# Keyed scores in front of query-major scores: one reordering on TensorE in a pipelined attention kernel

## The reference

```python
Qh, Kh, Vh = (split_heads(Q), split_heads(K), split_heads(V))
scores = jnp.einsum('bhqd,bhkd->bhqk', Qh, Kh) / jnp.sqrt(jnp.float32(D))
scores = jnp.where(mask == 0, jnp.float32(-1000000000.0), scores)
attn = jax.nn.softmax(scores, axis=-1)
Z = jnp.einsum('bhqk,bhkd->bhqd', attn, Vh)
```

## Time and profile before

| | us |
|---|---|
| median of three runs | 1529.95 (1526.15 to 1530.41) |
| the profiled execution's own time | 1529.28 |
| its span, first to last instruction | 1527.4 |
| outside the span | 1.88 |
| TensorE busy with matmuls, over the span | 1186.4 |
| VectorE busy | 977.2 |
| ScalarE busy | 639.0 |
| GpSimd busy | 596.7 |

### The profile page before, as it was taken

One profiled execution on the slowest core, in us unless ns is written; L12 is line 12 of the kernel. 1 busy time (PEld: TensorE's weight loads), 2 busy tenths in 40 slices (PEclk: granted clock), 3 DMA queues, 4 the chain that ended last, 5 costly groups with the idle time before them and its releaser, 6 DMA issues. The chain is left out here.

```text
span 1527.4 us, 30086 instructions
## 1 busy us (share of the span) xinstructions
PE 1186.4 (78%) x9187; PEld 789.3 (52%) x9187; DVE 977.2 (64%) x4100; ACT 639.0 (42%) x1541; POOL 596.7 (39%) x1132
## 2 busy tenths in 40 slices
PE   3789989998365479999996395884658865999778
PEld 2455555554365245565553294763655642454455
DVE  5777777773566567787772674365655655776445
ACT  2355645444222145666654043330235431666422
POOL 3553478987243344455420443322430112321120
PEclk9699999999578579999998597776787895999889
DMA  6344665530022344455420125001220014341000
GB/s 185 118 129 141 207 183 169 182 122 3 32 60 61 104 127 124 137 168 168 147 82 11 40 57 176 0 15 34 62 76 1 0 39 135 101 123 43 2 0 28
DMA packets 140014, 137.35 MB, mean 90 GB/s; under 512 B 12288, under 2 KB 109184, under 8 KB 139728
## 3 DMA queue, kind: packets, MB, share of 16 engines
q1 hardware_dynamic: 131248, 110.88, 23.9%
q0 software_dynamic: 8608, 24.55, 5.0%
HBM read 83.58 MB, written 49.18 MB: 87 GB/s over the span
## 5 line engine op out<-in xcount | busy, mean ns | idle before, releaser
L762 ACT ACTIVATE L0a_Pr<-PS 128x512 f32<-128x512 f32 (+1 forms) x256 | 136.8, 547 | 137.5 <-PE PS L664 88.4
L762 ACT ACTIVATE L1a_Pr<-PS 128x512 f32<-128x512 f32 (+1 forms) x256 | 136.2, 547 | 100.5 <-PE PS L664 50.5
L479 POOL TENSOR_TENSOR L0a_PG<-L0a_Pr,L0a_G 128x512 f32<-128x512 f32 x80 | 105.7, 1325 | 25.6 <-issue 11.0
L885 DVE CUSTOM_DVE_ANT_0 L1a_junk<-PS,L1a_neg 128x256 bf16<-128x256 f32 x256 | 94.8, 420 | 29.7 <-PE PS L637 29.4
L637 PE MATMUL PS<-L0a_Kst,Qm 128*128 128x256 bf16 (+1 forms) x512 | 94.9, 272 | 16.8 <-DVE L0a_mx L885 9.9
L637 PE MATMUL PS<-L1a_Kst,Qm 128*128 128x256 bf16 (+1 forms) x512 | 94.7, 272 | 16.5 <-DVE L1a_mx L885 9.1
L885 DVE CUSTOM_DVE_ANT_0 L1a_junk<-PS,causal_q 128x128 bf16<-128x128 f32 (+1 forms) x256 | 78.5, 352 | 37.0 <-PE PS L637 36.3
L885 DVE CUSTOM_DVE_ANT_0 L0a_junk<-PS,causal_q 128x128 bf16<-128x128 f32 (+1 forms) x256 | 78.5, 352 | 36.7 <-PE PS L637 36.0
L888 DVE TENSOR_REDUCE L3x_mx<-PS 128x2 f32<-128x512 f32 x128 | 83.8, 685 | 24.5 <-PE PS L637 24.2
L659 PE MATMUL PS<-Qm,L0a_Kst 128*128 128x512 bf16 (+1 forms) x256 | 91.5, 357 | 9.3 <-DMA Qm<-L0a_mT 6.6
L885 DVE CUSTOM_DVE_ANT_0 L0a_junk<-PS,L0a_neg 128x256 bf16<-128x256 f32 x192 | 72.9, 418 | 37.0 <-PE PS L637 36.5
(11 more groups left out here) (739 smaller groups left out, 3183.4 us busy)
## 6 DMA issues: line engine op xcount, KB each, us to landing
Qm<-q_image SPq DMA_DIRECT2D x160, 128.0 KB
sorted_in<-zeros POOLq DMA_DIRECT2D x16, 516.0 KB, 4.3
L0a_Kst<-k_image SPq DMA_DIRECT2D x64, 128.0 KB
ffn_w_<-L_ffn POOLq DMA_DIRECT2D x32, 256.0 KB, 3.5
L1a_Kst<-k_image SPq DMA_DIRECT2D x64, 128.0 KB
ffn_w_<-L_ffn SPq DMA_DIRECT2D x16, 256.0 KB, 6.3
L3x_Kst<-k_image SPq DMA_DIRECT2D x32, 128.0 KB
k_image<-L0a_kpart SPq DMA_DIRECT2D x16, 192.0 KB, 2.6
```

The source lines that it names most:

```text
L479: g.tensor_tensor(PG[:, V_ % GATED_RING, :].rearrange("p (h q) -> p h q", h=2), Pr[:, V_ % RING, :].rearrange("p (h q) -> p h q", h=2), G[ ...
L762: a(Pr[:, V_ % RING, 0:2 * nq], PS[:, T_BANK + v % 2, 0:2 * nq], ACT.Exp, scale=SCALE)\
L885: ins = v.tensor_tensor_reduce(junk[:, tt, par, 0:nk], scored[:, par], off, 1.0, LOWEST, ALU.add, ALU.max, mx[:, i % 2, tt, par, hp:hp + 1])
```

## The change

In each step of the loop on TensorE, the call of `keyed_scores` is put in front of that of `scores`. Nothing is added or removed, the waits inside the two functions move with them, and the programs of the other engines stay as they are.

```diff
+                    i, v = unit(n, TLAG)
+                    if i is not None:
+                        keyed_scores(i, v)
                     i, u = unit(n, 0)
                     if i is not None:
                         scores(i, u)
-                    i, v = unit(n, TLAG)
-                    if i is not None:
-                        keyed_scores(i, v)
                     i, x = unit(n, PV_LAG)
                     if i is not None and x % 4 == 0:
                         times_v(i, x // 4)
```

## The result

| | before | after |
|---|---|---|
| median of nine runs each, us | 1526.15 (1521.06 to 1530.41) | 1536.02 (1531.82 to 1540.96) |
| ratio after to before | | 1.0069, 95% interval 1.0048 to 1.0090 |
| the profiled execution's own time, us | 1529.28 | 1536.02 |
| its span, us | 1527.4 | 1534.2 |
| VectorE busy, us | 977.2 | 997.3 |

The kernel became 0.7% slower where I had put 1527.3, 0.2% faster than the median of 1529.95 that I started from. The surprise of the page is in VectorE's row: its program did not change, and it is busy for 20.1 us more. To find the place I took each item's period, from the end of its last E to the end of the next item's last E (items 0 to 7 are L0a, 8 to 15 L0x; the groups are counted from the end of their first E).

What follows compares the result with a forecast made beforehand. TensorE's own work was taken to bound the mixed stretches. Terms 2.7 + 0.6 - 1.9 + 1.7 + 0.9 - 1.3 + 0 gave 2.7 us gained: 1529.28 to 1526.6, or 1527.3 with the median 0.67 higher; range 1518 to 1537.

Steps and rivals of the forecast that it cites:

- The bound: Mixed attention stretches: TensorE's own work sets the pace, so only what alters its waits can move the end.
- the cost of the change: Mixed steps: no matmul added, S and T keep 640 each and their durations, and the switch costs nothing in itself.
- The third rival: Nothing moves: stream and waits turn as one, GpSimd holds L0x and gives back the rest; 1530 us, chance 0.05.
- The loop turns without moving: Mixed steps: waits of S and T neither removed nor doubled, only slightly changed; +2.7, +0.6 and -1.9 us.
- `pick_heads`: L602's wait for the copy `Osb`, which moves earlier with T: +1.7 us in causal blocks, +0.9 in L1x and L3x.
- `turn_attended`: L610's wait for `A`, whose chain starts at S and comes 0.22 us later in six cases of L0a and L1a: -1.3 us.
- The first T: First T of an item waits for the transfer of maxima, S now behind it: +0.9 and -0.9, together 0 us.
- 15.84 within 0.2: Sign: the 15.84 us between like steps of a late L0a item would stay within 0.2 of that.
- T's waits for `Pr` grown by 10 us or more: Sign in the trace after that was to prove the rival that S stands behind T's waits.
- the second rival: S stands behind T's waits: E's arrival doesn't move while S's place does; 1540.7 us, chance 0.15.
- S's total far below 56 us: Sign: with T's waits small, it would prove that T fills S's waits, a rival at 1519.6 us, chance 0.20.

Runs made afterwards that it cites:

- e1: The swap everywhere except in steps whose keyed scores belong to L0x, against the kernel before: 1523.08 us, ratio 1.0002.
- e3: Old order, GpSimd's gate products cut to 8 columns (part of the gating left out), against the kernel before: 1516.01 us, ratio 0.9946.
- e4: New order, GpSimd's gate products cut to 8 columns (part of the gating left out), against the kernel before: 1515.43 us, ratio 0.9955.
- e14: New order, GpSimd's gate products replaced by about equally long fills that read nothing, against the kernel before: 1523.56 us, ratio 0.9983.
- e15: Old order, GpSimd's gate products replaced by the same fills that read nothing, against the kernel before: 1522.17 us, ratio 0.9978.
- e5: New order, VectorE's gate product put ahead of the step's row maximum, against the kernel before: 1522.12 us, ratio 0.9981.
- e6: Old order, VectorE's gate product put ahead of the step's row maximum, against the kernel before: 1529.13 us, ratio 1.0034.
- e7: New order, VectorE's gate product one step later, still behind the row maximum, against the kernel before: 1527.30 us, ratio 1.0016.
- e8: Old order, VectorE's gate product one step later, still behind the row maximum, against the kernel before: 1526.41 us, ratio 1.0009.
- e12: Built on e4, one VectorE product in each of two items followed by five copies into spare tiles; against the kernel before: 1519.28 us, ratio 0.9968.
- e9: New order, GpSimd's expert weight transfers issued four steps later, against the kernel before: 1528.89 us, ratio 1.0034.
- e10: Old order, GpSimd's expert weight transfers issued four steps later, against the kernel before: 1511.99 us, ratio 0.9923.

## Why the prediction was wrong

- **The bound.** Right outside L0x. I called TensorE the pace of all mixed stretches, and noted GpSimd's 130.1 of 150 us in L0x only as a second engine. That it reads SBUF beside VectorE's product I didn't ask. The time of 1536.02 lies inside the range that I gave (1518 to 1537), on the side of slower: that is the width of the range, and no credit to the mechanism.
- **The step that failed** is the cost of the change: "S and T keep their counts (640 each) and durations", and nothing of any other engine's durations. L897 stands in no step of it: what the new order does to its length was put at nothing, without a reason. It went from 39.5 to 57.9 us, held M so that S waited up to 3.22 us, and behind that wait the clock fell. The third rival said that GpSimd "holds L0x (130.1 of 150) and gives back the rest"; the reverse happened: the two engines got in each other's way, and the cost moved to VectorE, which TensorE waits for (GpSimd's 80 products sum to 104.3 us, from 106.0).
- **The loop turns without moving** (+2.7, +0.6, -1.9). The mechanism held: e1 gives 1.0002, the items of L0a move by half a microsecond at most in both directions (item 5, where I had named 15.84 within 0.2, has 15.54), and items 33 to 35 of L3x are 0.21 us shorter each. The single terms are too small for what was measured.
- **`pick_heads`** (+2.6 in all). Right in the trace: L602's waits, 3.0, 4.7 and 1.8 us in the earlier trace rows, are no longer among the waits of these stretches. No time came of it that could be measured.
- **`turn_attended`** (-1.3). Right in sign, larger in number: L610 waits 4.1 us in 7 times and 5.8 in 13, from 2.5 in 3 each.
- **The first T** (0). In the case I worked through, the wait went from 0.82 to 0.67 us, 0.15 less, where I had 0.2. Over the groups it grew, from 8.2 to 9.1 us in the first, and in the second this term was mis-sized: the first T of item 17 waits 1.79 us, from 1.05. Of the changed kernel's TensorE and clock there:

```profile
...
575.88 0.39 PE L659 MATMUL PS<-Qm,L1a_Kst 128*128 128x512 bf16 x1 [1.79 <-DMA Qm<-L1a_mT]
...
```
```profile
576.00:580.00 4.00, 4.00 (x33) 2.45 (x32) 2.14 (x16) 1.79 (x3) 1.15 (x3) 0.61 0.64 202
580.00:590.00 10.00, 8.92 (x86) 5.93 (x87) 6.73 (x41) 4.42 (x11) 2.70 (x8) 0.99 0.19 65
```

  Behind the idle 1.79 us the granted clock is 0.61 over 4 us, near its 1.2 GHz level, and 0.99, the 2.4 GHz level, again behind them. Item 17 is 1.53 us longer by it, of the second group's +2.3. The wait belongs to the new order: it is 1.68 to 1.99 us in all eight kernels that have the swap there and the weights at their old step, and 1.05 to 1.17 in the six with the old order. The fall of the clock is in two of the eight, this one and e1, with 19.16 and 19.22 us for item 17; the other six have 17.48 to 17.80, as before (17.63). So the wait alone costs nothing that can be measured, and the fall costs 1.6 us when it comes. What decides whether it comes was not settled. In the median of e1 no loss is left of it.
- **The signs that I named.** "T's waits for `Pr` grown by 10 us or more" was to prove the second rival. They grew from 1.8, 2.6 and 3.7 us to 4.3, 5.8 and 11.2, by 13.2 in all, and most in L3x, which ended 0.2 us earlier. There S waits 7.1 us less and T 7.5 us more: the wait changed its name. The sign was badly chosen, as a wait that moves from one instruction to another in the same loop costs nothing. "S's total far below 56 us" didn't come: 33.4 + 16.1 + 6.3 = 55.8.
- **The second rival** had a time nearest to the result (1540.7 against 1536.0), for a reason that e3, e4, e14 and e15 exclude. That is luck.
- **Not settled.** That the swap puts L897 at the start of GpSimd's products is in the traces (22 of 48 against 2, above); why it does is inferred: it brings E, which releases GpSimd's products, nearer, and M, behind which L897 stands, further off. e5 to e8 agree with that, but the arrivals were not worked out one by one. Nor is it settled why M had more slack in e12, nor why a product listed ahead of GpSimd's can be held by it.

## What to carry to other kernels

When two engines can hold each other up at SBUF in a stretch, as VectorE and GpSimd do here, durations are not constants: ask what a reordering on a third engine does to when they meet, even if their own programs stay. Read minimum, median and maximum of an instruction rather than its mean. When an instruction of the same shape grows between two versions, look at what lies beside it before the order itself is blamed. Read the clock behind a long wait of TensorE, too: here the slow stretch behind it cost half of what the wait did, on top of it. Equal waits that change their name in a loop that turns as a whole are not a loss.

## What the runs showed of the hardware

- A VectorE product of two SBUF inputs was held not for one GpSimd instruction but across two and the transfer issue between them: 4.13 us where it takes 0.68, ended 0.57 us after the second product. It is listed as starting 0.42 us before the first of these, beside the issue L495. Whether the issue or the product held it first was not told apart. In e9 a product of 3.79 us was held across four GpSimd instructions (L479, L534 twice, L479) with no issue among them.
- It goes the other way too: where VectorE's product is listed 0.11 us ahead of GpSimd's (before, at 222.91), VectorE's takes 0.69 us and GpSimd's 1.71 instead of 1.27.
- VectorE's row maximum, of PSUM and one SBUF input (L885), takes 0.41 to 0.43 us inside GpSimd's products and 0.39 to 0.43 outside them, and the product of two SBUF inputs takes 0.68 beside GpSimd fills of 1.27 us (e14).
- Behind TensorE's wait of 3.22 us in L0x the granted clock was 0.58 over 4.1 us (the 1.2 GHz level in most of it), and 1.00 again after that. The same fall stood behind the wait of 2.37 us in e7 and the five of 2.46 to 2.67 in e9; behind e12's 1.05 and 1.10 us the clock stayed at 1.00.
- Kernels with the same VectorE and GpSimd products in L0x, profiled in one execution each, have from none to five holds over 3 us (e9: five in a profile of 1536.9 us, with a median of 1528.89).
- With expert weights issued 0.32 us ahead of a small transfer that TensorE waits for, T came 0.8 us later than with the weights issued 5.4 us behind it (3.89 against 3.10 us from issue to T). It is a part of e10's 0.8%.
